# DLRM tower kernel: new tables of tile kinds and of gather places, and embedding rows written later in layer 2

## What is computed

```python
e = jnp.stack([tbl_0[ids[:, 0]], ..., tbl_38[ids[:, 38]]], axis=1)      # 1024 x 39 x 16
x0 = xk = e
for W, b in ((w0, b0), (w1, b1), (w2, b2)):
    z = relu(einsum('bhd,bkd,hks->bsd', x0, xk, W) + b[None, :, None])   # 128 rows
    # first 64 rows are the next xk, the others go out; of the last layer all 128 go out
logit = sum(concatenate(out rows), axis=-1)                              # over the 16 numbers
h = concatenate([logit, dense_ctx], axis=1)
h = maximum(h @ W_top1 + b_top1, 0)
h = maximum(h @ W_top2 + b_top2, 0)
y = h @ W_top3
```

## Time and profile before

| | |
|---|---|
| median of 3 runs | 1243.73 us (1243.71 to 1244.59) |
| the profiled execution | 1244.94 us, its span 1243.1 us |
| TensorE busy (matmul) | 1179.9 us, 95% of the span, granted clock 0.999 |
| VectorE busy | 1061.9 us, 85% |
| GpSimd busy | 1002.6 us, 81% |
| ScalarE busy | 580.7 us, 47% |
| chain that ended last | TensorE 69%, GpSimd 13%, VectorE 8% of the span |

### The profile page before, as it was taken

The page is one execution under the profiler, slowest core; times in us unless marked ns, Lnnn a source line. Parts: engine busy times, 40 slices in busy tenths (PEclk is TensorE's granted clock), DMA queues, the critical chain, the costliest instruction groups (busy, mean ns, idle before and its releaser), DMA issues.

```text
span 1243.1 us, 14868 instructions
## 1 busy us (share of the span) xinstructions
PE 1179.9 (95%) x3856; PEld 726.5 (58%) x3856; DVE 1061.9 (85%) x927; ACT 580.7 (47%) x563; POOL 1002.6 (81%) x629
## 2 busy tenths in 40 slices
PE   0289999999999999999999999999999999999999
PEld 0155666656565665656566565656656565666665
DVE  2278998989899898989889898998989898998984
ACT  1145444444545444454544445454444545444545
POOL 6678897998889899888989888888988889765651
PEclk9999999999999999999999999999999999999999
DMA  4785726365472626556262745637274563627000
GB/s 125 242 256 191 223 63 218 125 182 201 157 226 60 218 108 206 177 172 211 84 204 97 225 159 172 211 102 215 79 233 140 172 211 123 212 72 231 9 1 1
DMA packets 110269, 196.21 MB, mean 158 GB/s; under 512 B 52975, under 2 KB 64334, under 8 KB 110249
## 3 DMA queue, kind: packets, MB, share of 16 engines
q1 hardware_dynamic: 100009, 193.33, 47.2%
q0 software_dynamic: 10240, 2.64, 2.0%
HBM read 193.36 MB, written 12.78 MB: 166 GB/s over the span
## 4 chain that ended last, share of the span: by engine, by line
PE 69%; POOL 13%; DVE 8%; issue 6%; ACT 2%; DMA 2%; POOLq 0%; SPq 0%; DVEq 0%; ACTq 0%
PE acc L845 67%; POOL lo L464 7%; POOL emb L454 6%; DVE prod L706 3%; DVE lo L719 2%; ACT hi L556 2%; DVE acc L706 1%; DVE hi L716 1%; DMA x_tiles<-x_rows 0%; DMA x_rows<-x_rows 0%; DVE xk L706 0%; PE acc L925 0%; POOLq L163 0%; DMA x_rows<-emb 0%; ACT xk L522 0%
## 5 line engine op out<-in xcount | busy, mean ns | idle before, releaser
L706 DVE TENSOR_TENSOR prod<-x_tiles,xk 128x1024 f32<-128x1024 f32 (+2 forms) x643 | 757.5, 1215 | 123.9 <-PE acc L845 83.4
L464 POOL TENSOR_TENSOR lo<-prod,hi 128x1024 fp32r<-128x1024 f32 (+1 forms) x288 | 690.5, 2400 | 141.1 <-ACT hi L556 136.4
L845 PE MATMUL acc<-prod,wfull 128*128 128x512 f32 (+2 forms) x1408 | 660.6, 593 | 0.0
L556 ACT ACTIVATE hi<-prod 128x1024 fp32r<-128x1024 f32 (+1 forms) x291 | 308.4, 1060 | 406.3 <-DVE prod L706 322.4
L845 PE MATMUL acc<-hi,whi 128*128 128x512 f32 (+1 forms) x800 | 353.0, 441 | 57.7 <-ACT hi L556 57.6
L845 PEld LDWEIGHTS acc<-prod,wfull 128*128 128x128 f32 (+2 forms) x1408 | 266.8, 189 | 205.7 <-issue 177.4
L454 POOL DMA_INDIRECT emb<-table,block_idx x320 | 308.6, 964 | 69.3 <-issue 63.9
L845 PE MATMUL acc<-lo,whi 128*128 128x512 f32 (+1 forms) x736 | 316.1, 517 | 2.4 <-POOL lo L464 1.2
L845 PE MATMUL acc<-hi,wlo 128*128 128x512 f32 (+1 forms) x800 | 316.1, 395 | 0.0
L845 PEld LDWEIGHTS acc<-hi,whi 128*128 128x128 f32 (+1 forms) x800 | 150.9, 189 | 112.4 <-issue 72.2
L845 PEld LDWEIGHTS acc<-lo,whi 128*128 128x128 f32 (+1 forms) x736 | 138.3, 190 | 133.2 <-issue 104.0
(11 more groups left out here) (72 smaller groups left out, 163.4 us busy)
## 6 DMA issues: line engine op xcount, KB each, us to landing
x_tiles<-x_rows SPq DMA_DIRECT2D x304, 512.0 KB, 5.1
x_rows<-x_rows SPq DMA_DIRECT2D x16, 624.0 KB
x_tiles<-x_rows SPq DMA_DIRECT2D x32, 256.0 KB, 5.6
x_stack<-x_rows SPq DMA_DIRECT2D x48, 156.0 KB
emb<-table,block_idx POOLq DMA_INDIRECT x320, 3.8
x_rows<-emb SPq DMA_DIRECT2D x16, 152.0 KB, 3.3
x_tiles<-w SPq DMA_DIRECT2D x1, 768.0 KB, 6.1
x_tiles<-w SPq DMA_DIRECT2D x1, 704.0 KB, 8.6
```

The lines of the kernel that those rows point to most:

```text
L464: nc.gpsimd.tensor_tensor(lo[0:r, product_slot(j), :], prod[0:r, product_slot(j), :], hi[0:r, part_slot(j), :].bitcast(f32), ALU.subtract) ...
L556: nc.scalar.activation(hi[0:r, part_slot(j), :], held(n, parity, j)[0:r, :], ACT.Copy).then_inc(hi_ready, 1)
L706: nc.vector.tensor_tensor(held(n, parity, j)[0:r, :], in0, in1, ALU.mult).then_inc(product_ready, 1)
L845: mm = nc.tensor.matmul(z[:, c], w[0:r], part[0:r, c], start=first and i == 0, stop=last and i == len(weights) - 1)
```

## The change

Four tables and three places in the code are different.

- `KINDS`: a block has 20 F, 18 G, 7 D and 2 H tiles instead of 22, 18, 5 and 2. Layer 0 has 4 F and 3 G (5 and 2), layer 1 8 F, 7 G, 4 D, 1 H (8, 8, 3, 1), layer 2 8 F, 8 G, 3 D, 1 H (9, 8, 2, 1). The places differ too; layer 1 begins with a D tile, layer 0 with an F tile, and layer 2 ends with three F tiles. H stays at place 12.
- `GATHERS`: a list gives the number of gathers behind each subtraction of GpSimd. In layer 1 they are 1, 0, 3, 1, 0, 1, 3, in layer 0 none, in layer 2 0, 1, 0, 2, 1, 1, 1, 5. Before, there was one behind each of the eight in layer 1, two behind both of layer 0, and two behind each of the first four of layer 2.
- Start: 16 of block 1's gathers instead of 12 stand ahead of the first subtraction, and the other four behind layer 0's last one instead of behind both.
- `WRITE_AFTER` is 12 instead of 9.
- `SQUARE`, the place of layer 0's tile 0 in its weights, is 3 instead of 0, so one weight load is cut in two.

The numbers of slots and the evacuations' places stay.

```diff
-KINDS = ["GFFGFFF", "GFDGF" * 2 + "GFHGF" + "GFDGF", "GFFGF" + "GFFGD" + "GFHGF" + "GFDGF"]
+KINDS = ["FGFGGFF", "DFGDGFFGFDGFHGGFDFGF", "GFGGFGDFGDGFHGFDGFFF"]
...
+SQUARE = (SPLITS[0] + FULLS[0]).index(0)
...
-                sp.dma_start(w0t_stage[0:ROWS0, 1:T0 - 1, :], w0t[:, 1:T0 - 1, :]).then_inc(w0_loaded, 16)
+                if SQUARE:
+                    sp.dma_start(w0t_stage[0:ROWS0, 0:SQUARE, :], w0t[:, 0:SQUARE, :]).then_inc(w0_loaded, 16)
+                sp.dma_start(w0t_stage[0:ROWS0, SQUARE + 1:T0 - 1, :], w0t[:, SQUARE + 1:T0 - 1, :]).then_inc(w0_loaded, 16)
...
-            WRITE_AFTER = 9
+            WRITE_AFTER = REST - 1
...
-            gather(1, 0, 12)
+            gather(1, 0, 16)
...
-                between = max(1, len(tiles) - (4 if l == 2 else 0))
-                for i, t in enumerate(tiles):
-                    subtract(n, at + t)
-                    if m is not None and i < between:
-                        gather(parity, start + i * (stop - start) // between,
-                               start + (i + 1) * (stop - start) // between)
...
+                for i, j in enumerate(tiles):
+                    subtract(n, j)
+                    if m is not None:
+                        gather(parity, start, start + gathers[i])
+                        start += gathers[i]
...
+            GATHERS = [[0, 0, 0], [1, 0, 3, 1, 0, 1, 3], [0, 1, 0, 2, 1, 1, 1, 5]]
```

More of the change, by code:

```diff
@@ L311, in load_weights @@
                 sp.dma_start(w0f_stage[0:LAST0, len(FULLS[0]) - 1, :], w0[0:LAST0, T0 - 1, :]).then_inc(w0_loaded, 16)
-                sp.dma_start(w0t_stage[0:ROWS0, 1:T0 - 1, :], w0t[:, 1:T0 - 1, :]).then_inc(w0_loaded, 16)
+                if SQUARE:
+                    sp.dma_start(w0t_stage[0:ROWS0, 0:SQUARE, :], w0t[:, 0:SQUARE, :]).then_inc(w0_loaded, 16)
+                sp.dma_start(w0t_stage[0:ROWS0, SQUARE + 1:T0 - 1, :], w0t[:, SQUARE + 1:T0 - 1, :]).then_inc(w0_loaded, 16)
                 sp.dma_start(w0t_stage[0:LAST0, T0 - 1, :], w0t[0:LAST0, T0 - 1, :]).then_inc(w0_loaded, 16)
                 sp.wait_ge(w0_cleared, 1)
-                sp.dma_start(w0t_stage[FIELDS:ROWS0, 0, :], w0t[FIELDS:ROWS0, 0, :]).then_inc(w0_loaded, 16)
+                sp.dma_start(w0t_stage[FIELDS:ROWS0, SQUARE, :], w0t[FIELDS:ROWS0, SQUARE, :]).then_inc(w0_loaded, 16)
                 for l, b in enumerate((b0, b1, b2)):
@@ L472, in _, with layer @@
             take_indices(1, 1, reuse=False)
-            gather(1, 0, 12)
-            def layer(n, l, m=None, parity=0, gathers=(0, 0)):
-                at, tiles = (L0, L1, L2)[l], [t for t, k in enumerate(KINDS[l]) if k == "G"]
-                start, stop = gathers
-                between = max(1, len(tiles) - (4 if l == 2 else 0))
-                for i, t in enumerate(tiles):
-                    subtract(n, at + t)
-                    if m is not None and i < between:
-                        gather(parity, start + i * (stop - start) // between,
-                               start + (i + 1) * (stop - start) // between)
-            GATHERS = {1: (0, 8), 0: (8, 12), 2: (12, PAIRS)}
-            layer(PROLOGUE, 0, 1, 1, (12, PAIRS))
+            gather(1, 0, 16)
+            def layer(n, l, m=None, parity=0, gathers=()):
+                tiles = [j for j in range((L0, L1, L2)[l], (L0, L1, L2)[l] + len(KINDS[l])) if KIND[j] == "G"]
+                assert m is None or sum(gathers) == 0 or len(gathers) == len(tiles)
+                start = 0 if l == 1 else sum(GATHERS[1]) if l == 0 else PAIRS - sum(GATHERS[2])
+                for i, j in enumerate(tiles):
[4 more added lines that the diff above has]
+            GATHERS = [[0, 0, 0], [1, 0, 3, 1, 0, 1, 3], [0, 1, 0, 2, 1, 1, 1, 5]]
+            assert sum(map(sum, GATHERS)) == PAIRS
+            for j in [j for j in range(L0, L2) if KIND[j] == "G"]:
+                subtract(PROLOGUE, j)
+            gather(1, 16, PAIRS)
             take_indices(2, 0)
@@ L670, in _ @@
         def _(dve):
-            nc.vector.memset(w0t_stage[:, 0, :], 0.0).then_inc(w0_cleared, 1)
+            nc.vector.memset(w0t_stage[:, SQUARE, :], 0.0).then_inc(w0_cleared, 1)
             nc.vector.memset(direct2[:, :], 0.0).then_inc(direct2_cleared, 1)
             dve.wait_ge(direct2_cleared, 1)
-            dve.wait_ge(w0_loaded, 6 * 16)
+            dve.wait_ge(w0_loaded, (6 + (SQUARE > 0)) * 16)
             n, f = len(SPLITS[0]), len(FULLS[0])
```

## The result

The changed kernel takes **1225.95 us** (median of 4 runs, 1225.6 to 1226.63), the kernel before on the same chip 1244.16 us (1243.71 to 1244.87). The ratio is 0.9854, 95% interval 0.9837 to 0.9871: 1.5% faster, 18.2 us. The profiled execution took 1225.93 us, its span is 1224.1 us, 19.0 less than the 1243.1 of before. The forecast was 1226.4 us.

A forecast was written before the change was run, and what follows sets the result against it. TensorE, busy 95% of the span, was taken as the bound, with GpSimd late once a block. Span 1243.1 - 11.1 (term 1) - 5.6 (term 2) - 1.5 (start) + 0.9 (tail) = 1225.8 us; median 1226.4 us, range 1221.5 to 1236.

The forecast's parts named there:

- term 2: GpSimd's late remainder in layer 2: spreading the gathers removes a 0.40 us wait in 14 blocks, -5.6 us.
- term 1: TensorE: two F tiles a block become D in 16 blocks, 1.72 - 1.374 us each, -11.1 us.
- The rival that a wait stays: GpSimd, three places with 0.4 to 0.8 us to spare: 5.6 us lost, 1232.0 us, up to 1236; chance 0.16.
- the signs that the forecast named: Trace: period 70.5 to 70.8, 1280 F records, no GpSimd-released TensorE piece, stack copy idle for VectorE, first matmul at 51.7.
- The transfers: SyncE's write and tile loads: write 14 us later, 1.5 to 5 us to spare and three more before TensorE; cost 0.
- point of decision at VectorE: Rows for layer 0: lateness decides when write-to-last-tile takes some 5 us more than 26.2; costs TensorE beyond 8.
- rows late: Layer 0 waits for its tiles each block, slower than before; 1271 us at 3 us lost; chance 0.05.
- VectorE: 58 operations a block, 65.5 us of 70.5: costed at nothing, cover 5 us a block; 0.8 us lost at `HELD2`.
- The forecast's rival for this case: VectorE or ScalarE late at layer 0's end, so the two gains do not come: 1243 us; chance 0.05.
- Start: Layer 0 of block 0 begins with an F tile, first matmul at 51.7 instead of 52.88: -1.5 us beyond term 1.
- Tail: Last block: +1.1 us for a VectorE remainder, +1.5 for a slow SBUF one, about -1.7 in TensorE's last layer; together +0.9.
- The page's matmul gap: TensorE rival: F against split differs by two gaps, 0.458 us, so term 1 is 14.7 us: 1222.8 us; chance 0.02.

The follow-up runs named there:

- The gathers alone: Kernel before with its old tile kinds, but gathers spread, rows written behind place 12 and the new start: 1238.52 us, ratio 0.9946.
- the gathers early: Changed kernel's new tile kinds with gathers placed early as before and rows written behind place 9: 1347.6 us, ratio 1.0819.
- four copies instead of one: Changed kernel with the copies of the rows in HBM made four times a block, one after the other: 1326.2 us, ratio 1.0648.

## Why the prediction was right

**The block, -1.09 forecast, -1.05 measured** (-1.11 in the first 13). Both terms are shown by a run. The gathers alone gave 0.37 us a block, against 0.40 for term 2; the kinds gave 0.68, against 0.69 for term 1, and taking one D back cost 0.32. From all records, a D tile for an F tile is 4 x 0.429 - 6 x 0.231 = 0.33 us, so the 0.346 of term 1 was some 5% too large: 0.229 us was read between ten matmuls in a row, and the mean over the blocks is 0.231. The same difference, over a block's matmuls of split tiles, and 1.37 written for 6 x 0.229, are the 0.25 us that the forecast's sum left unexplained. It was not a wait, and so could not have gone. The block was to be 70.5 to 70.8; it is 70.76 in the loop and 70.83 with the step behind it. The rival that a wait stays was wrong: the only late remainder is hidden. With the gathers early the loss was 8 us a block. Of the signs that the forecast named, the 1280 records of F tiles are there and ScalarE's copy of the stack still waits for VectorE (16.9 us in the loop); the first matmul is at 48.97 us instead of 51.7, which the start explains.

**The transfers.** The forecast had the write 1.6 us into the block and the last tile 26.2 us behind it, with 1.5 to 5 us to spare at VectorE and 3 more at TensorE. The last tile was in fact down some 23 us behind the write (the loads go out 10.0 us behind it instead of 13.0, and take 8.8 us at most behind the last issue at 581.6), and the room is 7.6 to 9.0 us. Counted from 26.2 us that is 4 to 5.5, so the forecast's upper end and its point of decision at VectorE were right, and it is the chain that was shorter. Its second half was wrong: TensorE had some 0.8 us of cover, not 3. The rival "rows late" was priced right in kind; four copies instead of one show it.

**VectorE: the step that was mis-sized without showing in the time.** The forecast costed its two more operations at nothing with "5 us a block" of cover, which was 70.5 less 65.5. But a sum of durations is no cover when the engine must also stop: 2.8 us a block at slots and `HELD2`, and 0.1 to 0.25 us at each of some twelve more places, 2.1 us in all. The stop at `HELD2` was forecast at 0.8 us and was 1.16. The next operation would not have been free: it cost 17.5 us in all. The forecast's rival for this case had the right price (1243 us; 1243.5 to 1244.5 were measured, one tile further on) but looked for it at layer 0's end, with 0.05 us to spare there, while none of that was seen in the changed kernel: ScalarE's rounding there ends in time, and TensorE waits for nothing.

**Start, -1.5 forecast, -2.9 measured up to the first evacuation of layer 2: right by luck** (the first block's part of term 1, some 0.7, should be in it too). Timeline, VectorE and TensorE, as the earlier trace rows:

```profile
47.61 3.85 DVE L710 TENSOR_TENSOR prod<-x_tiles,xk 117x1024 f32<-117x1024 f32 x3 [23.99 <-DMA x_tiles<-x_rows]
```

```profile
48.97 3.60 PE L849 MATMUL acc<-prod,wfull 117*128 117x512 f32 x4 [48.97 <-DVE prod L710]
```

The step from product to first matmul shrank from 2.45 to 1.36 us, as the F tile at the head was to bring. The product itself was 2.8 us earlier, which the forecast hadn't: it waits for transfers, and in the traces of the experiments with more or fewer D tiles, whose starts are alike, it stands at 48.3, 48.5 and 50.4, so this part can't be put down to the change. Without it nearly nothing is left. From the first product to the first evacuation of layer 2, before and after (us, busy by engine, then the granted clock, 0.98 and 0.96):

```profile
50.43:146.31 95.88, 88.57 (x272) 53.22 (x273) 78.97 (x69) 42.10 (x40) 76.59 (x51) 0.98 0.70 233
```

```profile
47.61:143.43 95.82, 89.68 (x281) 54.76 (x282) 82.44 (x71) 45.19 (x43) 78.55 (x52) 0.96 0.67 226
```

Of the 2.2 us that the forecast had here with term 1, 1.3 went to the clock. In both traces TensorE stands idle for some 5 us ahead of layer 1 and then is granted half its clock, after the change for longer: an F tile with two `lo` matmuls takes 4.13 us from 68.84 on, where before it took 2.82 from 73.27 on and takes 2.18 at full clock. Two kernels with the new start and eight D tiles have the shorter stretch, so it isn't shown that the change brings the longer one. The rest was not followed.

**Tail, +0.9 forecast, -1.4 measured.** From the last evacuation of layer 2 before it to the dense part (1164.07) it took 28.97 us and before 28.79: +0.18. But the mark itself is late, by 71.82 - 70.76 = 1.06 us after and by 72.08 - 71.87 = 0.21 before; with that, VectorE's delay is +1.0 us, as forecast (+1.1), only that most of it stands in the row above the tail. From the dense part to the end it took 1.55 us less, beside the 1.7 forecast for the last layer. The other +1.5 was for a slow remainder more; none of the three is slow. From the trace of before, GpSimd beside the slow one of the earlier trace rows:

```profile
1199.69 2.38 POOL L464 TENSOR_TENSOR lo<-prod,hi 128x1024 fp32r<-128x1024 f32 x1 [1.32 <-ACT hi L556]
```

And of after, VectorE and GpSimd at one such place:

```profile
1181.98 1.22 DVE L723 TENSOR_TENSOR lo<-prod,hi 128x1024 fp32r<-128x1024 f32 x1
```

```profile
1182.10 3.37 POOL L467 TENSOR_TENSOR lo<-prod,hi 128x1024 fp32r<-128x1024 f32 x1 [1.11 <-ACT hi L560]
```

Before, VectorE's remainder began at 1200.41, inside GpSimd's, and lasted to 1203.15, 1.08 us behind GpSimd's end at 1202.07. After, VectorE's began first; it took its 1.22 us, and GpSimd's, which takes 2.40 alone, took 3.37. So whichever starts second of the two stands until the first is through. This is what the Trainium skill, "SBUF — State Buffer" (Who interferes with whom), says of two such instructions: they contend for one lock, and the order in which they come decides who waits. The trace agrees. The trace of before has the other order too: at 1213.62 VectorE's remainder came first and took 1.22 us, and GpSimd's from 1213.74 took 3.35. The forecast had that they contend, not who pays: of VectorE's three remainders there one (1177.33) has no subtraction of GpSimd beside it, two (1181.98, 1191.40) began first, and GpSimd paid.

**The page's matmul gap** (the Trainium skill, "TensorE: Matmul & The Clock Gate", Back-to-back issue gap). The forecast took 216 ns from it, which the section gives for an isolated matmul; for a stream of weight loads and matmuls, as here, it gives 131 ns, by which term 1 would be, as an estimate from that page of the Trainium skill, 32 x 2 x 0.131 = 8.4 us instead of 13.8. The trace agrees with neither for the whole: a record of an F tile stands 0.429 us behind the one before, which is twice 0.214 and near the first figure, and a matmul of a split tile 0.231 behind the one before. With 0.33 us a tile, as measured, term 1 is 10.6 us.

**How near it came.** Span 19.0 us less, against 17.3 forecast; the medians 18.2 less. The blocks came as forecast. Start and tail did not: without the earlier first product the start gave 0.1 us where 2.2 were forecast, and the tail, with the late mark put right, 0.5 less where 0.5 more was forecast (0.9 and its part of term 1). These two misses and the 2.8 us of the earlier product nearly cancel. That the median lies within 0.5 us of the forecast is luck; that it lies near is not.
